# A transformer stack on one Trainium2 core: the first attention group's maximum products start two pairs later, and the second group's stack is loaded between stores

## The chip, the cores and the metric

One Trainium2 chip, one core. The metric is the device time of one execution in microseconds (us), taken as the median of several runs. The kernel before the change has a median of 1548.95 us over three runs (1544.71 to 1552.33).

## What is computed

Four attention blocks follow each other on x of shape (2, 1024, 256), with a context of 77 tokens a batch. The change touches the first block alone, and of it the projections and the first two groups of heads:

```python
b, t, d = x.shape                                     # 2, 1024, 256; 16 heads of width 16
qkv = (_ln(x, g1, be1) @ w_qkv + b_qkv).reshape(b, t, 3, h, dh)
ckv = (context @ w_ckv + b_ckv).reshape(b, s, 2, h, dh)
k = jnp.concatenate([k_self, k_ctx], axis=1)
v = jnp.concatenate([v_self, v_ctx], axis=1)
scores = jnp.einsum('bthd,bshd->bhts', q, k) * scale
scores = jnp.where((j >= t) | (j <= i), scores, -jnp.inf)   # causal on own keys, the context is always seen
attn = jax.nn.softmax(scores, axis=-1)
attn_out = jnp.einsum('bhts,bshd->bthd', attn, v).reshape(b, t, d)
x = x + attn_out
```

What follows (a feed-forward block, three attention layers over the context and themselves, a windowed attention and a last encoder layer) is left as it is.

## The kernel before, in words

The program is written engine by engine, with semaphores between the engines, and in stages: at the end of a stage every engine drains and waits for the others (`next_stage`). The stage of this change is the first, called the front here, and the beginning of the second, the attention of the first block (`at0`).

**The front** makes 18 *features* (q and k of the 2048 tokens and the keys of the context, each 128 features wide and up to 512 tokens long) and 18 *values* (v of 128 tokens each). They alternate: feature i and value i are pair i, and the items are numbered 0 to 35, feature i being number 2i. The table of TensorE's order is `front_tensor`, that of the others `front_scalar`, `front_vector`, `front_gpsimd` and `front_sync`.

- A feature is four matmul passes of 512 columns on TensorE (L570). ScalarE rounds it to bf16 (L607), VectorE takes the remainder (L642), ScalarE rounds that (L588), GpSimd takes what is still left (L681). The three bf16 parts lie in a ring of 6 buffers, and SyncE stores them to DRAM (L696). ScalarE waits for the buffer's earlier store.
- A value is four passes of 256 columns (L576), one addition on VectorE (L637) into a ring of 5 buffers, and a store (L699). VectorE waits for the buffer's earlier store.
- Into this are woven the transposes of the normalised x (L557, `TURNS_AT`, the last two at numbers 22 and 24).

**The maximum products.** The softmax of this kernel subtracts row maxima that are found beforehand. For each group of 4 heads there are 43 products of q and k (7 over the context, L1199, and 36 over the own keys, L1210) in banks 6 and 7 in turn: product n may start when VectorE has reduced product n-2 (`chunk_free`; L1427, L1438, L1442). A last transpose on TensorE (L1215) and four small VectorE instructions turn the maxima into three bf16 rows (`neg_max_parts`). SyncE sends these rows into the q stack of the group by DMA (L1066, `send_maximum_rows`), and the scores of the group (L1243) wait for them. For group 0 all 43 products lie in the front: from pair `MAXIMA_FROM // 2` on, `MAXIMA_EACH` of them a pair. `front_maxima(A, pair, place)` names the one of a place: place 0 stands before the feature product, place 1 behind it, place 2 behind the value product. Whatever is left comes after pair 17. VectorE follows the same table.

**The loads.** A group's stack (q, k and context keys, three parts each; pieces 0 to 2 of `load_group`, L1001 to L1004, nine DMAs) and its values (piece 3, L1007 and L1008) are read back from DRAM. Group 0's stack is asked for after number 9. Its values, all of group 1 and then the rows of group 0 are asked for at the end of the front, behind the last store. All of it goes through SyncE's one queue, in this order. Groups 2 and on, and the weights of the next blocks, follow in the next stage (`attention_sync`).

Of the kernel before, what the change touches and what calls it, by code (L numbers as in the profile page):

```python
# [182 lines left out]
def build(nc, a, out):  # L183
    with ExitStack() as ctx:
        program(nc, ctx, a, out)


def program(nc, ctx, a, out):
# [97 lines left out]
    def need(e, sem, value):  # L286

        if not (isinstance(value, int) and value <= 0):
            e.wait_ge(sem, value)
# [202 lines left out]
    def turn_ctx_tensor(e, s, src, ready=None, value=1):  # L492
        if ready is not None:
            e.wait_ge(ready, value)
        for b in range(B):
            for k in range(KT):
                e.transpose(PS[:, 6, (k * B + b) * P:(k * B + b) * P + SC], src[0:SC, b, k * P:(k + 1) * P],
                            ID[0:SC, 0:SC]).then_inc(s.turned, 1)
# [15 lines left out]
    RING, V_RING = len(P3), len(VT)  # L514

    def part(it, i, k):

        return P3[i % RING][:, 2 - k if it.reverse else k, 0:it.n]
# [2 lines left out]
    FRONT_SCR = [WA[:, 2560 + CH * i:2560 + CH * (i + 1)] for i in range(2)]  # L521
    TURNS_AT = {0: [(0, 0), (0, 1)], 2: [(1, 0)], 4: [(1, 1)], 14: [(2, 0)], 16: [(2, 1)], 22: [(3, 0)], 24: [(3, 1)]}
    STATISTICS_AT, NORMALISE_AT = {6: 2, 14: 3}, {8: 2, 16: 3}
    MAXIMA_FROM, MAXIMA_EACH = 20, 3

    def in_order(items):

        for i, (it, v) in enumerate(zip(*items)):
            yield True, it, i
            yield False, v, i  # L530

    def front_maxima(A, pair, place):

        items = numbered(A, 0, -1)[0]
        n = max(pair - MAXIMA_FROM // 2, 0) * MAXIMA_EACH
        if pair == len(items0[0]):
            return items[n:]
        return items[n + place:n + place + 1] if pair >= MAXIMA_FROM // 2 else []

    def turn_bank(n):  # L540

        return PS[:, (3, 7)[n % 2] if n < 4 else 3, :]

    def turn_needs(n):

        return n - 1 if n < 4 else 3 if n == 4 else n

    def front_tensor(e, s, tn, tnc, nm, items, A):

        turn_ctx_tensor(e, tnc, CTXN)  # L550
        for number, (is_feature, it, i) in enumerate(in_order(items)):
            for c, k in TURNS_AT.get(number, []):
                n = KT * c + k
                e.wait_ge(nm.normed, c + 1)
                need(e, tn.taken, turn_needs(n))
                for j in range(4):
                    m = e.transpose(turn_bank(n)[:, j * P:(j + 1) * P], FRONT_ROWS[:, 4 * c + j, k * P:(k + 1) * P], ID[:, :])  # L557
                m.then_inc(tn.turned, 1)
            if it.chunk is None:
                e.wait_ge(tnc.taken, 1)  # L560
                e.wait_ge(ld.w_ctx, 16)
            else:
                e.wait_ge(tn.taken, KT * (it.chunk + 1))
                e.wait_ge(ld.w0, 16)
            if is_feature:
                for x in front_maxima(A, i, 0):
                    attention_chunk(e, A, *x, 0, -1)
                need(e, s.left, i - 2)
                for j, (l, r) in enumerate(it.mms):
                    m = e.matmul(PS[0:P, i % 3, 0:it.n], l, r, start=(j == 0), stop=(j == len(it.mms) - 1))  # L570
                m.then_inc(s.product, 1)
            else:
                need(e, stored0.v_taken, i - 1)
                for sl, mms in it.mms:
                    for j, (l, r) in enumerate(mms):
                        m = e.matmul(PS[0:it.p, 4 + i % 2, sl], l, r, start=(j == 0), stop=(j == len(mms) - 1))  # L576
                m.then_inc(s.v_product, 1)
            for place in ((1,), (2,))[not is_feature]:
                for x in front_maxima(A, i, place):
                    attention_chunk(e, A, *x, 0, -1)  # L580
        for x in front_maxima(A, len(items[0]), 0):
            attention_chunk(e, A, *x, 0, -1)
# [36 lines left out]
    def front_vector(e, s, nm, items, A):  # L619

        statistics, scales, _ = ln_steps(e, nm, X, "layer", 1e-5, arrived=ld.x_chunks)

        def normalise_here(c):
            scales(c)
            e.drain()
            for t in range(4 * c, 4 * c + 4):
                z = e.tensor_scalar(FRONT_ROWS[:, t, :], X[:, t, :], RS[:, t:t + 1], NB[:, t:t + 1], ALU.mult, ALU.add)
            z.then_inc(nm.normed, 1)

        def value(v, i):  # L630
            e.wait_ge(s.v_product, i + 1)
            if i >= V_RING:
                e.wait_ge(value_stored[i % V_RING], 16 * (i // V_RING))
            dst = VT[i % V_RING][0:v.p, 0:512].rearrange("p (h w) -> p h w", w=32)[:, :, 0:16]
            src = PS[0:v.p, 4 + i % 2, 0:D].rearrange("p (h w) -> p h w", h=16)
            r = v.row[0:v.p, :].rearrange("p (h w) -> p h w", h=16)
            e.tensor_tensor(dst, src, r, ALU.add).then_inc(stored0.v_taken, 1)  # L637

        def remainder(it, i):
            e.wait_ge(s.first_part, i + 1)  # L640
            need(e, stored0.split, i - 1)
            e.scalar_tensor_tensor(RBUF[:, i % 2, 0:it.n], PS[:, i % 3, 0:it.n], it.bias, part(it, i, 0),  # L642
                                   ALU.add, ALU.subtract).then_inc(s.left, 1)

        def maxima(pair, place):
            for w, dg, k, n, bank in front_maxima(A, pair, place):
                e.wait_ge(A.s.chunk_ready, n + 1)
                if w in "AL":
                    maximum_part(e, A, k, n, bank, 0, FRONT_SCR, w == "L")
                else:  # L650
                    maximum_split(e, A, 0, bank)
        for c in range(2):
            statistics(c)
            normalise_here(c)
        e.wait_ge(ld.rows0, 16)
        late = []
        for number, (is_feature, it, i) in enumerate(in_order(items)):
            if number in STATISTICS_AT:
                statistics(STATISTICS_AT[number])
            if number in NORMALISE_AT:  # L660
                normalise_here(NORMALISE_AT[number])
            if number < MAXIMA_FROM:
                (remainder if is_feature else value)(it, i)
                continue
            if is_feature:
                maxima(i, 0)
            for make, *of in late:
                if make is (remainder if is_feature else value):
                    make(*of)
            late = [x for x in late if x[0] is not (remainder if is_feature else value)]  # L670
            late.append((remainder if is_feature else value, it, i))
            maxima(i, 2 - is_feature)
        for make, *of in late:
            make(*of)
        maxima(len(items[0]), 0)
# [7 lines left out]
    def stored_after(e, feat, val):  # L683

        for u in range(RING):
            need(e, part_stored[u], 16 * ((feat + RING - 1 - u) // RING))
        for u in range(V_RING):
            need(e, value_stored[u], 16 * ((val + V_RING - 1 - u) // V_RING))
# [13 lines left out]
    def ones_sync(e, A):  # L702

        e.dma_start(ONES_ROWS, ONEB[0:M_ROWS * A.nh * TB, :]).then_inc(A.s.ones, 16)
        e.wait_ge(A.s.ones, 16)
        for u in range(A.slots):
            e.dma_start(slot16(A, u)[1][K16:K16 + M_ROWS, :, P:P + T], ONES_ROWS.rearrange("(r h t) n -> r h (t n)", r=M_ROWS, h=A.nh))\
                .then_inc(A.s.ones, 16)

    def front_sync(e, items, A):  # L710

        ones_sync(e, A)
        for number, (is_feature, it, i) in enumerate(in_order(items)):
            store_item(e, is_feature, it, i)
            if number == 2 * FIRST_FEATURES - 1:
                e.wait_ge(A.s.cleared, 1)
                for u in range(FIRST_FEATURES):
                    e.wait_ge(part_stored[u], 16)
                load_group(e, A, 0, 0, (0, 1, 2))
        stored_after(e, len(items[0]), len(items[1]))  # L720
        e.wait_ge(A.s.ones, 16 * (1 + A.slots))
        load_group(e, A, 0, 0, (3,))
        load_group(e, A, 1, 1)
        send_maximum_rows(e, A, 0)

    def project(stage):
# [2381 lines left out]
    part_stored, value_stored = stored0.parts, stored0.values  # L3108
# [45 lines left out]
    def _(e):  # L3154
        nxt = lambda: next_stage(e, "sync")
        load_sync(e)
        nxt()
        front_sync(e, items0, at0)
        nxt()
        attention_sync(e, at0)  # L3160
# [204 lines left out]
```

## Time and profile before

| what | value |
| --- | --- |
| median of three runs | 1548.95 us (1544.71 to 1552.33) |
| the profiled execution's own time | 1548.56 us |
| its span in the trace | 1546.8 us |
| granted TensorE clock over the span | 0.94 of full speed |
| TensorE busy | 1333.0 us (86%) |
| VectorE busy | 1069.4 us (69%) |
| ScalarE busy | 739.4 us (48%) |
| GpSimd busy | 538.2 us (35%) |
| front and first rows, until group 0's first scores start | 103.38 us |

The busy shares are averages over stages with different limits. The part of interest is the first 110 us. The timeline of an engine gives for each row the start, the time and the instruction, and in brackets the idle time before it with what ended it. Adjacent rows overlap where instructions are pipelined: the distance between starts is what an instruction costs, the time in its row also holds its latency. A view by windows gives for each stretch the busy time of every engine, the granted clock as a share of full speed, the share of time that the 16 DMA engines were busy (it may pass 1.00 a little), and GB/s.

### The profile page before, as it was taken

Reading aid. Unit: us, or ns where it says so; the run is one execution under the profiler, and the core shown is the slowest. Engines: PE = TensorE matmul, PEld = TensorE weight load, DVE = VectorE, ACT = ScalarE, POOL = GpSimd, SP = SyncE. Lnnn points to the kernel's source line nnn. Section 1 sums busy time; section 2 is a strip of 40 time slices with the busy share of each in tenths; the row PEclk is TensorE's granted clock in tenths of the full one; section 3 lists DMA queues with packets and bytes.
Section 4 is the critical chain, followed back from the end, with each engine's and each line's share of the span. In section 5 each row is a group of like instructions: output and inputs, shape, how many; then the busy total and the mean of one; then the engine's idle time right before and its main releaser. Section 6 shows DMA issues by size and latency. Waiting matters only on the chain.

```text
span 1546.8 us, 21751 instructions
## 1 busy us (share of the span) xinstructions
PE 1333.0 (86%) x7242; PEld 768.5 (50%) x7242; DVE 1069.4 (69%) x2667; ACT 739.4 (48%) x1030; POOL 538.2 (35%) x462
## 2 busy tenths in 40 slices
PE   7859999998699879879999979799998789788897
PEld 4413333332388756644444356344433577445796
DVE  6558888886654377667577767675777888676654
ACT  4325565567776345523334445233443634245664
POOL 3211111112410042207876621267864257001212
PEclk9869999999899998979999999799999889799999
DMA  6794333300000001553430317704400020630001
GB/s 201 198 201 122 63 66 65 64 8 2 28 1 1 1 1 67 159 170 69 96 87 22 104 49 213 186 16 96 96 28 12 17 35 32 155 65 3 1 1 55
DMA packets 80022, 110.39 MB, mean 71 GB/s; under 512 B 16713, under 2 KB 55811, under 8 KB 78119
## 3 DMA queue, kind: packets, MB, share of 16 engines
q1 hardware_dynamic: 79910, 109.00, 28.6%
q8 instruction: 58, 0.95, 0.3%
q14 instruction: 54, 0.43, 0.1%
HBM read 70.62 MB, written 37.83 MB: 70 GB/s over the span
## 4 chain that ended last, share of the span: by engine, by line
PE 41%; POOLq 19%; DVE 16%; issue 12%; ACT 6%; DVEq 3%; DMA 2%; SPq 1%; POOL 1%; ACTq 0%
POOLq L1157 18%; PE banks L1268 6%; PE banks L1610 5%; PE banks L1625 5%; PE banks L1210 4%; PE banks L1243 3%; PE banks L2196 3%; PE banks L2226 2%; DVE mask_rows L1438 1%; PE banks L570 1%; PE banks L1221 1%; DVE max_parts L1442 1%; PE banks L2744 1%; DVE max_parts L1427 1%; ACT x_feat L1403 1%
## 5 line engine op out<-in xcount | busy, mean ns | idle before, releaser
L1403 ACT ACTIVATE x_feat<-banks,key_bias 128x1024 f32<-128x1024 f32 x160 | 176.6, 1114 | 266.9 <-PE banks L1250 210.8
L1156 POOL TENSOR_TENSOR x_feat<-x_feat 128x1024 f32<-128x1024 f32 (+1 forms) x112 | 243.1, 2170 | 98.3 <-ACT x_feat L1403 90.1
L1210 PE MATMUL banks<-stacks 128*128 128x512 f32 (+4 forms) x640 | 225.1, 400 | 35.7 <-DVE max_parts L1431 12.2
L1268 PE MATMUL banks<-x_feat,v_group 128*32 128x512 f32 (+4 forms) x1312 | 232.6, 571 | 8.3 <-ACT x_feat L1403 4.7
L1403 ACT ACTIVATE x_feat<-banks 128x1024 f32<-128x1024 f32 (+2 forms) x224 | 178.8, 841 | 112.2 <-PE banks L1243 111.1
L1210 PEld LDWEIGHTS banks<-stacks 96*128 96x128 bf16 (+1 forms) x640 | 79.1, 139 | 219.0 <-DVE max_parts L1431 90.8
L1243 PE MATMUL banks<-stacks 99*128 99x512 bf16 (+3 forms) x512 | 131.2, 347 | 23.1 <-ACT x_feat L1403 12.3
L1180 POOL TENSOR_SCALAR_AFFINE_SELECT x_feat<-x_feat 128x256 f32<-128x256 f32 x128 | 53.4, 420 | 249.2 <-ACT x_feat L1403 247.5
L1431 DVE CUSTOM_DVE_ANT_0 scratch<-banks,mask_rows 128x512 f32<-128x512 f32 x128 | 88.1, 689 | 51.4 <-PE banks L1210 51.2
L1249 PE MATMUL banks<-stacks 128*128 128x512 f32 x256 | 111.5, 436 | 9.5 <-DMA stacks<-neg_max_parts_r 9.5
L1610 PE MATMUL banks<-stacks 128*128 128x512 f32 x384 | 102.7, 407 | 9.8 <-DVE stacks L1592 8.9
L1250 PE MATMUL banks<-stacks 96*128 96x512 f32 x256 | 103.8, 405 | 0.0
L1625 PE MATMUL banks<-stacks 128*128 128x256 f32 x768 | 102.1, 284 | 0.0
L1625 PEld LDWEIGHTS banks<-stacks 128*128 128x128 f32 x768 | 99.1, 191 | 3.9
L1442 DVE TENSOR_REDUCE max_parts<-banks 128x1 f32<-128x512 f32 x128 | 84.4, 687 | 12.7 <-PE banks L1210 11.8
L1427 DVE TENSOR_REDUCE max_parts<-banks 128x5 f32<-128x385 f32 (+2 forms) x104 | 54.0, 547 | 45.0 <-PE banks L1199 30.0
L1431 DVE CUSTOM_DVE_ANT_0 w_even<-banks,mask_rows 128x512 f32<-128x512 f32 x112 | 77.0, 688 | 11.6 <-PE banks L1210 11.3
L1610 PEld LDWEIGHTS banks<-stacks 128*128 128x128 f32 x384 | 71.1, 197 | 23.3 <-issue 9.6
L2196 PE MATMUL banks<-x_feat,w_odd 128*128 128x512 f32 x160 | 80.6, 632 | 0.8 <-ACT x_feat L2315 0.8
L1268 PEld LDWEIGHTS banks<-x_feat,v_group 128*32 128x32 f32 (+1 forms) x1312 | 41.5, 119 | 78.3 <-issue 53.1
L1249 PEld LDWEIGHTS banks<-stacks 128*128 128x128 f32 x256 | 50.0, 195 | 60.3 <-issue 42.6
L1243 PEld LDWEIGHTS banks<-stacks 99*128 99x128 bf16 x512 | 44.9, 99 | 61.4 <-ACT x_feat L1403 29.5
(308 smaller groups left out, 2461.8 us busy)
## 6 DMA issues: line engine op xcount, KB each, us to landing
stacks<-q_parts_r SPq DMA_DIRECT2D x18, 512.0 KB, 7.1
stacks<-k_parts_r SPq DMA_DIRECT2D x18, 512.0 KB, 10.7
q_parts_r<-stacks SPq DMA_DIRECT2D x16, 512.0 KB, 3.1
k_parts_r<-stacks SPq DMA_DIRECT2D x16, 512.0 KB, 3.4
v_group<-v SPq DMA_DIRECT2D x14, 512.0 KB, 15.1
stacks<-q_parts SPq DMA_DIRECT2D x16, 384.0 KB, 5.1
stacks<-q_parts SPq DMA_DIRECT2D x16, 256.0 KB, 7.4
w_even<-in_w SPq DMA_DIRECT2D x4, 1024.0 KB, 16.0
```

The costliest lines, as they stand in the source:

```text
L1156: e.tensor_tensor(total, total, p, ALU.add)
L1157: e.drain().then_inc(s.tile_summed, 1)
L1210: m = e.matmul(PS[:, bank, at:at + wide], q[0:rows, h, qt * P:(qt + 1) * P], keys[0:rows, h, k0:k0 + wide], start=True, stop=True, skip_gr ...
L1243: m = e.matmul(o, k[0:rows, head_of_k(A, r, h), k0:k0 + P], q[0:rows, h, qs], start=True, stop=True, skip_group_check=True)
L1249: e.matmul(o, ka[:, hk, ks], qa[:, h, qs], start=True, stop=False)
L1250: m = e.matmul(o, kb[0:96, hk, ks], qb[0:96, h, qs], start=False, stop=True)
L1268: m = e.matmul(PS[w * h:w * (h + 1), bank, t.q0:CH], V[:, h, :], PB[:, t.index % 2, h // 2, h % 2, 0:CH - t.q0], start=t.first, stop=t.las ...
L1403: e.activation(dst, PS[:, 2 * (st % 2):2 * (st % 2) + 2, 0:CH - t.q0], ACT.Exp, scale=A.scale, bias=bias).then_inc(s.p_ready, 1)
L1431: e.tensor_tensor_reduce(scratch, PS[:, bank, :], MB[:, k0:k0 + CH], 1.0, LOWEST, ALU.add, ALU.max, maxp[:, h, qt, half:half + 1]).then_in ...
L1610: mm = e.matmul(PS[:, i % 3, :], w[:, k, ms], x[:, c % 2, k, :], start=k == 0 and w is w1h and x is XH, stop=k == KT - 1 and w is w1l)
L1625: mm = e.matmul(o, h[:, i % 4, ts], w[:, m, :], start=m == 0 and t % 2 == 0 and h is HID_H and w is w2h, stop=m == MT_F - 1 and h is HID_L ...
L2196: m = e.matmul(PS[:, n % 2, :], left, right, start=k == 0, stop=k == KT - 1)
```

## The change

Two tables of numbers change: the maximum products start at pair 12, four a pair (places 2 and 3 both stand behind the value product), where they started at pair 10, three a pair. 24 of the 43 lie in the pairs before and after. And SyncE asks for the three pieces of group 1's stack after the stores of numbers 24, 27 and 30, for group 0's values after number 32; at the end only group 1's values stand between the last store and the rows of group 0.

```diff
-    MAXIMA_FROM, MAXIMA_EACH = 20, 3
+    MAXIMA_FROM, MAXIMA_EACH = 24, 4
...
-            for place in ((1,), (2,))[not is_feature]:
+            for place in ((1,), (2, 3))[not is_feature]:
                 for x in front_maxima(A, i, place):
                     attention_chunk(e, A, *x, 0, -1)
...
-            maxima(i, 2 - is_feature)
+            for place in ((1,), (2, 3))[not is_feature]:
+                maxima(i, place)
...
+    NEXT_STACK_AT, FIRST_VALUES_AT = (24, 27, 30), 32
...
+            if number in NEXT_STACK_AT:
+                load_group(e, A, 1, 1, (NEXT_STACK_AT.index(number),))
+            if number == FIRST_VALUES_AT:
+                for u in range(V_RING):
+                    e.wait_ge(value_stored[u], 32)
+                load_group(e, A, 0, 0, (3,))
         stored_after(e, len(items[0]), len(items[1]))
         e.wait_ge(A.s.ones, 16 * (1 + A.slots))
-        load_group(e, A, 0, 0, (3,))
-        load_group(e, A, 1, 1)
+        load_group(e, A, 1, 1, (3,))
         send_maximum_rows(e, A, 0)
```

TensorE's order from pair 10 on, before. L570 is a feature product, L576 a value product, L557 a transpose of x, L1199 a maximum product over the context (up to five small matmuls):

```order
26 L576 MATMUL banks<-w_even,x_feat 128x256 x2
27 L1199 MATMUL banks<-stacks 128x77 x5
28 L570 MATMUL banks<-x_feat,w_even 128x512 x2
29 L1199 MATMUL banks<-stacks 128x77 x5
30 L576 MATMUL banks<-w_even,x_feat 128x256 x2
31 L1199 MATMUL banks<-stacks 128x77 x5
```

and in the changed kernel, where L1199 has become L1207:

```order
26 L576 MATMUL banks<-w_even,x_feat 128x256 x2
27 L570 MATMUL banks<-x_feat,w_even 128x512 x2
28 L576 MATMUL banks<-w_even,x_feat 128x256 x2
29 L557 MATMUL banks<-ident,w_even 128x128 x4
30 L570 MATMUL banks<-x_feat,w_even 128x512 x2
31 L576 MATMUL banks<-w_even,x_feat 128x256 x2
32 L557 MATMUL banks<-ident,w_even 128x128 x4
33 L1207 MATMUL banks<-stacks 128x77 x5
```

The first product that reads group 0's stack stood ahead of pair 10 and now stands ahead of pair 12: two features, two values and both last transposes have moved in front of it.

TensorE's order around pair 14, before (L1210 is a maximum product over own keys):

```order
44 L570 MATMUL banks<-x_feat,w_even 128x512 x2
45 L1210 MATMUL banks<-stacks 128x512
46 L576 MATMUL banks<-w_even,x_feat 128x256 x2
47 L1210 MATMUL banks<-stacks 128x512 x2
48 L570 MATMUL banks<-x_feat,w_even 128x512 x2
```

and in the changed kernel (L1218 is what L1210 was):

```order
43 L570 MATMUL banks<-x_feat,w_even 128x512 x2
44 L1218 MATMUL banks<-stacks 128x512
45 L576 MATMUL banks<-w_even,x_feat 128x256 x2
46 L1218 MATMUL banks<-stacks 128x512 x3
47 L570 MATMUL banks<-x_feat,w_even 128x512 x2
```

Between a value product and the next feature product stood two maximum products, and now stand three, in two banks.

SyncE's order at the end of the front, before:

```order
56 L699 DMA v<-v_group 128x4x128 [waits set2_40]
57 L1007 DMA v_group<-v 128x1024 [waits set2_34,set2_35,set2_33,set2_36,set2_32,set2_37,set2_31,set2_38,set2_30,set2_27,set2_29,set2_28]
58 L1008 DMA v_group<-v 77x128
59 L1001 DMA stacks<-q_parts 48x4096
...
67 L1004 DMA stacks<-kctx_parts 16x4x77
68 L1007 DMA v_group<-v 128x1024
69 L1008 DMA v_group<-v 77x128
70 L1066 DMA stacks<-neg_max_parts 1x32x128 [waits set2_8,set2_18,set2_15]
```

and in the changed kernel:

```order
67 L700 DMA v<-v_group 128x4x128 [waits set2_40]
68 L1015 DMA v_group<-v 128x1024 [waits set2_34,set2_35,set2_33,set2_36,set2_32,set2_37,set2_31,set2_38,set2_30,set2_27,set2_29,set2_28]
69 L1016 DMA v_group<-v 77x128
70 L1074 DMA stacks<-neg_max_parts 1x32x128 [waits set2_8,set2_18,set2_15]
```

Eleven DMAs that stood between the last store and group 0's rows have moved up among the stores; two are left there.

## Rows read from the trace of the kernel before

**Rows 1.** Chain of waits in order of time: start us, us, what

```profile
40.00 7.89 DMA stacks<-kctx_parts
...
94.86 0.29 DVE neg_max_parts L1466
...
96.55 6.69 DMA stacks<-neg_max_parts
103.38 1.03 PE banks L1243 x2
```

**Rows 2.** Timeline of TensorE, around pairs 8 to 10, 12 to 14 and 17

```profile
34.99 0.60 PE L557 MATMUL banks<-ident,w_even 128*128 128x128 f32 x4
35.43 1.88 PE L570 MATMUL banks<-x_feat,w_even 128*128 128x512 f32 x4
...
38.01 1.88 PE L570 MATMUL banks<-x_feat,w_even 128*128 128x512 f32 x4
39.73 1.03 PE L576 MATMUL banks<-w_even,x_feat 128*128 128x256 f32 x4
48.02 0.48 PE L1199 MATMUL banks<-stacks 96*128 96x77 bf16 x5 [7.27 <-DMA stacks<-kctx_parts]
...
58.05 1.96 PE L570 MATMUL banks<-x_feat,w_even 128*128 128x512 f32 x4
...
61.36 1.88 PE L570 MATMUL banks<-x_feat,w_even 128*128 128x512 f32 x4
63.08 0.38 PE L1210 MATMUL banks<-stacks 96*128 96x512 bf16 x1
63.30 1.03 PE L576 MATMUL banks<-w_even,x_feat 128*128 128x256 f32 x4
64.16 0.60 PE L1210 MATMUL banks<-stacks 96*128 96x512 bf16 x2
...
74.35 1.88 PE L570 MATMUL banks<-x_feat,w_even 128*128 128x512 f32 x4
```

**Rows 3.** Timeline of VectorE: one pair's share, and four products of the tail

```profile
63.50 0.69 DVE L1442 TENSOR_REDUCE max_parts<-banks 128x1 f32<-128x512 f32 x1 [0.21 <-PE banks L1210]
64.11 0.41 DVE L637 TENSOR_TENSOR v_group<-banks,rows_even 128x256 f32<-128x256 f32 x1
...
69.21 0.74 DVE L642 SCALAR_TENSOR_TENSOR y_tok<-banks,cols,y_tok 128x512 f32<-128x512 f32 x1
...
80.56 2.87 DVE L1442 TENSOR_REDUCE max_parts<-banks 128x1 f32<-128x512 f32 x4
```

**Rows 4.** Windows: PE, PEld, DVE, ACT, POOL busy, PEclk, DMA share, GB/s

```profile
40.00:84.00 44.00, 34.22 (x140) 18.21 (x138) 28.85 (x73) 12.96 (x21) 11.54 (x10) 0.84 0.75 207
85.00:105.00 20.00, 8.03 (x24) 2.02 (x25) 9.10 (x35) 0.52 (x1) 2.05 (x4) 0.50 1.04 181
```

**Rows 5.** The instructions of L1066, the rows' DMAs, over the whole program

```profile
DMA to landing us min/median/max: 1.7/1.8/6.7
```

**Rows 6.** Timeline of SyncE's queue: start and time of an issue

```profile
81.34 0.53 SPq L699 DMA_DIRECT2D v<-v_group  x1
89.95 0.42 SPq L1007 DMA_DIRECT2D v_group<-v  x1
...
95.24 1.91 SPq L1066 DMA_DIRECT2D stacks<-neg_max_parts  x3
```

**Rows 7.** DMA issues at 41.7 to 42.2 us: KB each, us to landing

```profile
v<-v_group SPq DMA_DIRECT2D x1, 256.0 KB, 7.9
```

**Rows 8.** Windows as in rows 4: where the granted clock falls or stays

```profile
55.00:75.00 20.00, 20.00 (x84) 11.53 (x83) 17.10 (x43) 8.23 (x14) 6.46 (x6) 1.00 0.62 193
78.00:80.00 2.00, 0.39 (x1) 0.10 (x1) 2.00 (x9) 0.63 (x1) 0.95 (x2) 1.00 0.67 200
80.00:82.00 2.00, 1.60 (x3) 0.30 (x3) 1.90 (x7) 0.00 (x0) 0.91 (x1) 0.62 0.93 288
1368.00:1412.00 44.00, 36.28 (x392) 18.43 (x392) 29.23 (x74) 21.29 (x20) 0.00 (x0) 1.00 0.20 40
```

## The prediction

> **What bounds the kernel now.** The page gives TensorE 86% of the span and VectorE 69%, but the change touches only the first 104 us, so the chain of waits of that stretch comes first [rows 1]. The reader is to see two DMAs in it: TensorE stands until 48.02 for the last piece of group 0's stack, and again until 103.38 for the three bf16 rows of the maxima, whose last DMA needs 6.69 us. Next comes TensorE's timeline [rows 2], for the first wait (7.27 us) and for what a pair costs, then VectorE's [rows 3] for its share. SyncE's queue and the landing times [rows 5 to 7] show what stands in front of the rows. The windows [rows 4, 8] show how full the DMA engines are, and when the granted clock falls.
>
> The front is one chain: TensorE and VectorE share its end, the attention starts only when it is over, and a group's start depends on the one before. Nothing later waits for a fixed time. I therefore take whatever moves the first scores (103.38) as moving the end of the kernel by the same amount.
>
> **Part 1, the start of the products.** From row to row a feature costs TensorE 1.72 us (38.01 to 39.73), a maximum product over own keys 0.22 (63.08 to 63.30), a value 0.86 (63.30 to 64.16), a group of four transposes 0.44 (34.99 to 35.43) [rows 2]. Value 9 ends at 39.73 + 0.86 = 40.6. Instead of standing until 48.02, TensorE now does pairs 10 and 11 and both last transposes: 2 x 2.58 + 2 x 0.44 = 6.0 us, to 46.6. Then it meets the same wait, now 1.4 us, since the loads of group 0 are issued where they were. The first product starts at 48.0 again and feature 12 at 48.2, where it started at 58.05: **9.85 us earlier**. In this are the 7.27 us of wait and the slow start after it, when TensorE's granted clock was at the half level, 1.2 GHz.
>
> Some of it is paid back at once. VectorE does value 10 before its first maximum, and value 10 and 11 wait for the stores of values 5 and 6, which are issued right behind the loads. That of value 6 goes out at 41.7 to 42.2 and lands 7.9 us after its issue [rows 7], at about 50, and that of value 5 some 1 us before it. I charge pairs 12 and 13 (seven of their eight products are the short ones over the context) with 3.9 and 3.7 us, where pair 12 took 3.31 (58.05 to 61.36) and pair 13 some 3.25: **+1.0 us**.
>
> **Part 2, four products a pair.** The number inside the pairs stays 24, the tail after pair 17 stays 20. In the four pairs 14 to 17 TensorE's own work grows to 1.72 + 0.86 + 4 x 0.22 = 3.46 us, from the 3.25 that a pair took ((74.35 - 61.36) / 4). But the order counts more. Three products now stand in a row between the value and the next feature, in two banks. The third may start when VectorE has reduced the first of them: that reduction starts 0.42 us behind its product (63.08 to 63.50), takes 0.69, and some 0.05 passes until TensorE goes on [rows 2, 3]. So from the first of the three to the end of the wait are 1.16 us, where there were 0.44, and a pair is 1.72 + 0.22 + 0.86 + 0.22 + 0.22 + 0.72 of waiting and first slot: 2.80 + 1.16 = 3.96. VectorE has 0.66 for the remainder (69.21's row, without its latency), 0.33 to 0.41 for the value and four times some 0.65: 3.6 to 3.7 at best. It arrives a little late at the first of the three, because the value's addition stands in front. I take 4.2. The bounds are 3.6 (VectorE never idle) and 4.5 (both engines' waits added). Over four pairs that is 4 x (4.2 - 3.25) = **+3.8 us**, between +1.4 and +5.0.
>
> The tail is 20 products paced by VectorE at about 0.7 each (2.87 for four, [rows 3]) before and after: no change. So the maxima of group 0 are ready 9.85 - 1.0 - 3.8 = **5.0 us earlier**, between 3.8 and 7.4, at about 90.1 instead of 95.1 (94.86 + 0.29, [rows 1]).
>
> **Part 3, the loads.** Before, eleven DMAs with 0.5 MB of group 0's values and 1.6 MB of group 1's stack, then 0.5 MB of group 1's values, were in the queue when the rows were issued at 95.24 [rows 6], and the DMA engines were busy throughout at 181 GB/s [rows 4]: 2.7 MB take about 15 us, from 84.66 to 99.6 at best. The rows, 8 KB each, landed after 6.69 us, while the median of all rows' DMAs is 1.8 [rows 5]. With only group 1's values in front, issued right behind the last stores, I take 1.8 for the last of them: **4.9 us earlier**, between 0 and 4.9.
>
> What the nine plus two moved DMAs cost where they now stand: SyncE spends about 0.45 us on each issue, some 5 us in all over 25 us, which delays a store by 1.4 us at most at a time. Features 12 to 17 wait for no store from there on, since their buffers' next turn would be feature 18. Values 15 to 17 wait for those of values 10 to 12, ten microseconds older. The DMA engines are the tight place: 44 us at a share of 0.75 are 33 us of work before [rows 4], and 2.1 MB at 181 GB/s add 12, so 45 us of work stand in the 39 us that the front now has until its last store. The last stores then land some 5 us late, at about 85, and group 1's values at about 88, still ahead of the rows at 90. I charge nothing, but the cover is only 2 us.
>
> **Sum**, against the profiled execution's own 1548.56 us: -5.0 - 4.9 = -9.9, which gives 1538.66, said as **1538.7 us**. The median of the runs, 1548.95, is 0.4 higher, so it serves as well.
>
> **The rivals.**
>
> *The rows stay late.* The oversubscribed DMA engines have not finished when the rows are issued, or group 2's load, issued right behind the rows as before, slows them. For it: the 45 us against 39, and the minimum cover of 2 us. Against it: the other groups' rows also have the next load right behind them and need 1.8 us. The time: only part 1 and 2 count, 1548.56 - 5.0 = 1543.6.
>
> *The clock falls in the pairs: slower than before.* The change takes TensorE from wholly busy (20.00 of 20 us, clock 1.00) to some 83% busy with a wait in each pair. Between 78 and 80 it was busy for 0.39 of 2 us, and from 80 on the clock came down to the half level, 1.2 GHz [rows 8]. At that level the work of a pair doubles to 6.9 us and, with the longer latencies, to about 7.6. From pair 12 on that would be 4 x 3.4 + 2 x 2 = 17.6 us more than in part 2, and 1548.56 - 9.9 + 17.6 = 1556.3. It decides from about the third slow pair on. Against it: from 1368 to 1412 TensorE was busy 36.28 of 44 us, 82%, with waits of the same kind on VectorE, and the clock stayed at 1.00 [rows 8]. The Trainium skill has a rule that speaks for this rival: its page TensorE: Matmul & The Clock Gate, section A second HAM failure mode: psum-queue depth-cycling, describes a kernel that cycled through banks, idled briefly between groups of matmuls and had its clock swing between the two levels. By that rule the time would be the rival's; the row at 82% disagrees, and I follow the row.
>
> *The gain is taken back behind the front.* The next stage, or a later one, ends on something that did not move, and the total stays at 1547 to 1549. For it speaks nothing that I see in the chain; against it, every later wait is on work of this same program.
>
> **How the numbers follow.** Both gains in full or nearly so (1536 to 1541.5): 0.60. Rows late: 0.20, 1543.6. Gain taken back or both terms small: 0.12, 1546 to 1549. Clock falls: 0.08, 1556.3. The forecast's own bounds are 1548.56 - 7.4 - 4.9 = 1536.3 and, with late rows, 1548.56 - 3.8 = 1544.8. The runs of before lie up to 4 us from their median, so the range is 1535 to 1546. About 0.5%, 7.7 us, is what a measurement can tell from no change here; the line is at 1541.2. Faster by more than that: most of the first case (1538.7 and below counts wholly, some of its upper part does not) and a quarter of the second, 0.60. Within 0.5%: 0.33. Slower: the last case, 0.07.
>
> **What the changed profile would show.** Right: the wait for group 0's stack is 1 to 2 us and stands ahead of feature 12 at 48; pairs 14 to 17 are 4.1 to 4.3 us apart, with a wait of some 0.7 us for a maximum ahead of each feature, at clock 1.00; the last of the four small instructions behind the maxima ends at 90; the rows land 1.8 us after their last issue and the first scores start at 93 to 94; the end of the kernel has moved by the same. Wrong: a landing of 4 us or more (rows late), a granted clock of 0.5 between 50 and 70 (clock), a wait of VectorE or ScalarE on a store behind pair 13, or a first score at 93 with an end above 1545.

## The result, and the profile after

The changed kernel's median is 1533.01 us over 5 runs (1530.10 to 1539.63), beside 1546.70 us of the kernel before (5 runs, 1543.30 to 1552.33): ratio 0.9918, 95% interval 0.9896 to 0.9940. It is faster, as forecast, but by more than forecast, and the time lies below the range of 1535 to 1546. The profiled execution's own time is 1534.61 us, its span 1532.9, against 1548.56 and 1546.8 before. Two more sets of runs of the same kernel gave the ratios 0.9924 (0.9902 to 0.9946) and 0.9944 (0.9926 to 0.9962).

The chain of waits of the changed kernel, start us, us, what. Line numbers have moved by up to 8:

```profile
38.84 9.53 DMA stacks<-kctx_parts
48.51 0.34 PE banks L1207 x5
...
92.29 1.84 DMA stacks<-neg_max_parts
94.27 1.02 PE banks L1251 x2
```

Against [rows 1] the load of group 0's stack is still in the chain, now with the transposes and four items done beside it. The last of the rows' DMAs takes 1.84 us, where it took 6.69. The first scores start at 94.27 instead of 103.38: 9.1 us.

TensorE's timeline, from pair 9 to pair 14:

```profile
39.70 1.03 PE L576 MATMUL banks<-w_even,x_feat 128*128 128x256 f32 x4
40.56 1.88 PE L570 MATMUL banks<-x_feat,w_even 128*128 128x512 f32 x4
...
46.16 0.60 PE L557 MATMUL banks<-ident,w_even 128*128 128x128 f32 x4
48.51 0.34 PE L1207 MATMUL banks<-stacks 96*128 96x77 bf16 x5 [1.75 <-DMA stacks<-kctx_parts]
48.68 1.96 PE L570 MATMUL banks<-x_feat,w_even 128*128 128x512 f32 x4
...
52.85 1.96 PE L570 MATMUL banks<-x_feat,w_even 128*128 128x512 f32 x4
...
56.71 1.88 PE L570 MATMUL banks<-x_feat,w_even 128*128 128x512 f32 x4
58.43 0.38 PE L1218 MATMUL banks<-stacks 96*128 96x512 bf16 x1
58.65 1.03 PE L576 MATMUL banks<-w_even,x_feat 128*128 128x256 f32 x4
59.51 0.60 PE L1218 MATMUL banks<-stacks 96*128 96x512 bf16 x2
60.77 0.38 PE L1218 MATMUL banks<-stacks 96*128 96x512 bf16 x1 [0.66 <-DVE max_parts L1450]
60.98 1.88 PE L570 MATMUL banks<-x_feat,w_even 128*128 128x512 f32 x4
...
69.62 1.88 PE L570 MATMUL banks<-x_feat,w_even 128*128 128x512 f32 x4
```

The wait for the stack has shrunk from 7.27 us [rows 2] to 1.75. Feature 12 starts at 48.68 (58.05 before), feature 17 at 69.62 (74.35 before). The third product in a row waits 0.66 us for VectorE ahead of the next feature: there are four such waits, of 0.66, 0.74, 0.66 and 0.66 us, ahead of features 15, 16 and 17 and at the beginning of the tail, and pairs 14 to 16 take (69.62 - 56.71) / 3 = 4.30 us each.

SyncE's queue at the end of the front:

```profile
77.30 0.63 SPq L700 DMA_DIRECT2D v<-v_group  x1
82.68 0.34 SPq L1015 DMA_DIRECT2D v_group<-v  x1
83.08 0.37 SPq L1016 DMA_DIRECT2D v_group<-v  x1
90.99 1.88 SPq L1074 DMA_DIRECT2D stacks<-neg_max_parts  x3
```

and the windows, columns as in [rows 4]:

```profile
57.00:74.00 17.00, 14.28 (x54) 7.42 (x52) 14.54 (x41) 4.82 (x8) 4.89 (x5) 1.00 1.05 260
80.00:90.00 10.00, 6.91 (x17) 1.25 (x15) 8.97 (x36) 0.00 (x0) 0.00 (x0) 0.50 0.29 91
```

The stores and loads fill the DMA engines from 57 to 74 (share 1.05; it was 0.62 from 55 to 75, [rows 8]). The last stores land 5.4 us after their issue at 77.3: the next issue, which waits for them, starts at 82.68. Before it was 3.3 us (81.34 in [rows 6] to an issue at 84.66). Group 1's values are asked for 7.9 us ahead of the rows. From 80 to 90 the DMA engines have a share of 0.29, and from 86 on, when those values have landed, they stand idle. TensorE is 84% busy from 57 to 74 and its granted clock stays at 1.00.

So all of the forecast is in the picture, and 9.1 us of the 13.9 between the two spans. The other 4.8 lie behind the first scores: from there to the end it was 1443.4 us before and 1438.6 now, in code that the change does not touch. That was the first question for the runs.

### The profile page after: what moved, and what is told of

Same layout as the page of the kernel before. It is cut to its first block, busy times and chain, and to the rows that moved or that the text cites. A ratio compares the mean times of both kernels' runs of the same rounds, so it can differ in the third digit from the quotient of the medians.

```text
span 1532.9 us, 21753 instructions
## 1 busy us (share of the span) xinstructions
PE 1328.7 (87%) x7242; PEld 766.8 (50%) x7242; DVE 1068.3 (70%) x2667; ACT 739.0 (48%) x1030; POOL 538.3 (35%) x462
## 4 chain that ended last, share of the span: by engine, by line
PE 40%; POOLq 19%; DVE 16%; issue 11%; ACT 6%; DVEq 3%; DMA 2%; SPq 1%; POOL 1%; ACTq 0%
POOLq L1165 19%; PE banks L1276 6%; PE banks L1618 5%; PE banks L1633 5%; PE banks L1218 4%; PE banks L2204 3%; PE banks L1251 3%; PE banks L2234 2%; DVE max_parts L1450 1%; DVE mask_rows L1446 1%; PE banks L1229 1%; ACT x_feat L1411 1%; DVE max_parts L1435 1%; PE banks L2222 1%; DVE scratch L1446 1%
## 5 line engine op out<-in xcount | busy, mean ns | idle before, releaser
L1218 PE MATMUL banks<-stacks 128*128 128x512 f32 (+4 forms) x640 | 224.2, 399 | 37.1 <-DVE max_parts L1439 12.4
L1218 PEld LDWEIGHTS banks<-stacks 96*128 96x128 bf16 (+1 forms) x640 | 78.8, 138 | 219.5 <-DVE max_parts L1439 91.8
L1439 DVE CUSTOM_DVE_ANT_0 w_even<-banks,mask_rows 128x512 f32<-128x512 f32 x112 | 77.0, 688 | 10.8 <-PE banks L1218 10.7
```

What stands on the lines that cost most here:

```text
L1218: m = e.matmul(PS[:, bank, at:at + wide], q[0:rows, h, qt * P:(qt + 1) * P], keys[0:rows, h, k0:k0 + wide], start=True, stop=True, skip_gr ...
L1439: e.tensor_tensor_reduce(scratch, PS[:, bank, :], MB[:, k0:k0 + CH], 1.0, LOWEST, ALU.add, ALU.max, maxp[:, h, qt, half:half + 1]).then_in ...
```

## The experiments

### The same two kernels again: does the part behind the front belong to the change?

No edit. The kernel before, with 12 runs of its own:

> The kernel before, unchanged, profiled and timed once more. Two theories on the 13.9 us between the two spans (1546.8 and 1532.9), of which the first scores of group 0 account for 9.1 (103.38 and 94.27). Theory A, chance episodes: the other 4.8 us are stretches at the half clock behind 1050 us (near 1060, 1124 and 1340) that differ from execution to execution. Then this profile has its first scores at 103.4 within 0.3, but the distance from the first scores to the end differs from the 1443.4 us of before by more than 1 us, the stretches of low clock behind 1050 us are not the same ones, and the runs' times follow their mean granted clock (a higher clock, a shorter time). Theory B, the change's own later gain: the distance from first scores to end is a property of the kernel, 1443.4 within 0.5 us again, with the same stretches of low clock. Ratio to before 1.000 within 0.002 by both.

Median 1546.42 us, ratio 0.9995 (0.9976 to 1.0015). The span of its profile was 1540.7 us, 6.1 less than the first profile of the same program. Yet its first scores came later:

```profile
106.61 1.01 PE L1243 MATMUL banks<-stacks 99*128 99x512 bf16 x2 [12.00 <-DMA stacks<-neg_max_parts]
```

The distance from the first scores to the end was therefore 1434.1 us, against 1443.4. One kernel draws numbers 9.3 us apart here, twice the 4.8 in question. The windows, columns as in [rows 4], show what differs. Here is a stretch of the first attention at the same distance behind the first scores, in the first profile:

```profile
383.38:398.38 15.00, 11.05 (x62) 2.72 (x54) 7.92 (x20) 14.42 (x23) 1.62 (x4) 0.89 0.00 0
```

and in this one:

```profile
386.61:401.61 15.00, 10.30 (x63) 2.28 (x62) 8.21 (x24) 14.96 (x23) 1.63 (x4) 1.00 0.00 0
```

The granted clock (0.89 against 1.00 of full speed) was at its half level for some 3 us in one execution and not in the other. The time at the half level behind the first scores, added up over windows of 5 us as twice (1 - clock) times 5 (the last window is not a full one), was 154.7 us in the first profile and 134.5 in the second. Over the 12 runs the time follows the mean clock: 1540.54 to 1544.74 us at 0.942 to 0.945, 1548.10 to 1552.02 us at 0.935 to 0.940. Theory A holds and theory B falls. Two parts of its text failed. The episodes do not lie only behind 1050 us: some 15 of the 20 us of half clock that the two profiles differ by lie ahead of it, like the stretch shown. And the first scores were not at 103.4 within 0.3, but 3.2 us later. The load of group 0 had landed 0.8 us later and the rows took 12.0 us instead of 9.8.

The changed kernel, with 6 runs:

> The changed kernel, unchanged, profiled and timed once more. Theory A (chance episodes): first scores at 94.3 within 0.3; distance from there to the end is another one than 1438.6 us, and over all runs the ratio to before comes near 1 - 9.1/1547 = 0.994. Theory B (a later gain that belongs to the change): the distance is again 1438.6 within 0.5, and the ratio again near 1 - 13.9/1547 = 0.991.

Median 1536.92 us, ratio 0.9924. First scores at 94.43, distance to the end 1442.4 us where the first profile had 1438.6: again theory A. The ratio lies between the two forecasts and tells nothing alone.

A third profile of each:

> The kernel before once more, one look. The wait for the rows was 9.8 us in its first profile and 12.0 us in its second. If it is a fixed 9.8 with one outlier, this one shows 9.8 within 0.3; if it varies with how the queue drains, anything from 9.5 to 12.5. Distance from first scores to the end: 1434 to 1444 us, and it follows the time at the half clock behind the first scores (154.7 us gave 1443.4, 134.5 us gave 1434.1: 0.46 us for each).

Time 1548.95 us, span 1547.2; the wait for the rows:

```profile
105.07 0.59 PE L1243 MATMUL banks<-stacks 99*128 99x512 bf16 x1 [10.70 <-DMA stacks<-neg_max_parts]
```

So this wait varies, 9.8, 12.0 and 10.7 us. Distance to the end 1442.1 us at 161.7 us of half clock; my factor of 0.46 us for each would have given 1446.6. Over all ten profiles at hand by then the distance rises by about 0.30 us for each microsecond at half clock, with a correlation of 0.91: it follows, not one for one.

> The changed kernel again, for more runs. If the gain is what the first scores show (105.0 us as a mean of three profiles of before: 103.38, 106.61, 105.07; 94.35 of two of the changed kernel), the ratio to before is near 1 - 10.7/1547 = 0.993, and first scores are at 94.3 again. If another part of the kernel gains as well, the ratio stays at 0.991 or below.

Median 1537.33 us (6 runs), ratio 0.9944. First scores:

```profile
93.50 1.01 PE L1251 MATMUL banks<-stacks 99*128 99x512 bf16 x2 [4.92 <-DMA stacks<-neg_max_parts]
```

The wait for the rows is 4.90, 4.93 and 4.92 us in the three profiles of the changed kernel: it no longer varies. The first scores are at 105.0 us (mean of three) before and at 94.1 now, 10.9 apart, and the distance from them to the end has the same mean in both, 1439.9 us before and 1439.7 now. All runs of the sets together have a mean of 1546.3 us before (67 runs, standard deviation 3.1) and of 1535.7 us now (17 runs, 3.3): 10.6 apart. The first scores' shift explains the whole change within the scatter.

### The two halves apart

Products as changed, loads as before (the edit against the kernel before, in part):

```diff
-    MAXIMA_FROM, MAXIMA_EACH = 20, 3
+    MAXIMA_FROM, MAXIMA_EACH = 24, 4
...
         load_group(e, A, 0, 0, (3,))
         load_group(e, A, 1, 1)
         send_maximum_rows(e, A, 0)
```

> Maximum products as in the changed kernel (from pair 12, four a pair), loads of group 0's values and of group 1 at the end as before. Theory of the two terms: pairs 14 to 17 are 4.3 us apart, the maxima are ready at 90.9, 4.2 us earlier than before (95.1), and the rows still land 6 to 7 us after the last issue, since the last store is some 4 us earlier as well and the queue ahead of them is the same: first scores at 99.2, gain 4.2 us, ratio 0.997. Rival (queue is not it): with these products the rows land in 1.8 us, first scores at 94.3. Rival that the half clock between 75 and 100 us carries part of the gain: first scores at 97 or less with rows still 6 us late.

Median 1540.67 us (8 runs), ratio 0.9957 (0.9937 to 0.9976). The end of the maxima and the first scores:

```profile
89.16 0.37 PE L1218 MATMUL banks<-ident,max_rows 128*32 128x128 f32 x1 [1.30 <-DVE max_rows L1450]
100.66 1.01 PE L1246 MATMUL banks<-stacks 99*128 99x512 bf16 x2 [11.13 <-DMA stacks<-neg_max_parts]
```

The last transpose behind the maxima starts at 89.16 as in the changed kernel (89.00); it was at 93.23, 94.24 and 94.00 in the three profiles of before, 93.8 in the mean. TensorE waits 11.1 us for the rows, the queue being what it was. Pairs 14 to 16 are 4.3 us apart. The first scores are 1.5 us later than forecast, because the last of the rows' DMAs took 8.08 us and not 6 to 7. Both rivals fall: the order of the products does nothing for the rows, and the half clock of the tail hides no gain.

Loads as changed, products as before (again against the kernel before, in part):

```diff
+            if number in NEXT_STACK_AT:
+                load_group(e, A, 1, 1, (NEXT_STACK_AT.index(number),))
...
         load_group(e, A, 1, 1, (3,))
         send_maximum_rows(e, A, 0)
```

> Loads as in the changed kernel, maximum products as before (from pair 10, three a pair). Theory of the two terms: TensorE waits 7.3 us for group 0's stack, the maxima are ready at 95.1 within 0.5, and the rows land 1.8 us after their last issue instead of 6.7: first scores at 98.5, gain 4.9 us, ratio 0.997. Rival (DMA engines overfull): pairs 12 to 17 are longer than 3.25 us because stores land late, and the maxima are ready at 96.5 or later. If theories of both terms hold, the two gains add up to the 9.1 of the changed kernel.

Median 1537.02 us (6 runs), ratio 0.9938 (0.9918 to 0.9958).

```profile
92.94 0.37 PE L1223 MATMUL banks<-ident,max_rows 128*32 128x128 f32 x1 [1.31 <-DVE max_rows L1455]
98.23 1.01 PE L1251 MATMUL banks<-stacks 99*128 99x512 bf16 x2 [4.92 <-DMA stacks<-neg_max_parts]
```

First scores at 98.23, forecast 98.5. Features 13 to 17 start 3.25 us apart (61.06 to 74.05 us), as before, and VectorE, ScalarE and GpSimd wait for no DMA from 38 to 90 us: the added 2.1 MB of loads among the stores delay no engine. They do delay the stores. The last of them is issued at 81.91 and has landed at 89.24 (81.34 and 84.66 before), but no engine needs it earlier. The rival of overfull DMA engines falls. The ratio of 0.997 was forecast from the first profile's rows and lies outside the interval; the gain is larger, because the rows of before waited longer in the other profiles.

Against the mean of before the first scores are 4.4 us earlier for the products alone and 6.8 for the loads alone, 11.2 together, and 10.9 for both: by the first scores the two terms add up. The runs' means do not show it as well. They are 6.1, 8.5 and 10.6 us below that of before, with a standard error of about 1 us each, so the halves sum to 4 us more than the whole.

### What is in front of the rows?

Against the changed kernel:

```diff
-            if number in NEXT_STACK_AT:
-                load_group(e, A, 1, 1, (NEXT_STACK_AT.index(number),))
...
-        load_group(e, A, 1, 1, (3,))
+        load_group(e, A, 1, 1)
         send_maximum_rows(e, A, 0)
```

> The changed kernel with group 1's stack asked for at the end again, behind the last store and ahead of the rows; group 0's values stay moved up. Theory (the rows wait for the bytes in front of them in the queue): with 2.7 MB asked for from 84.66, 85.70 and 80.54 on, the rows landed at 103.2, 106.5 and 100.5, that is 18.5 to 20.8 us later; 2.15 MB in front of them take 15 to 16.5 us from 82.2 on, so first scores at 97 to 99. Rival one (it is group 0's values that held the rows): first scores at 94.3. Rival two (it is only the stack, however much else is there): first scores at 100.5.

Median 1540.86 us (12 runs), ratio 0.9965 (0.9949 to 0.9980).

```profile
98.25 1.01 PE L1249 MATMUL banks<-stacks 99*128 99x512 bf16 x2 [8.44 <-DMA stacks<-neg_max_parts]
```

First scores at 98.25, within 97 to 99. The wait is 8.4 us with 2.15 MB in front, 9.8 to 12.0 with 2.7, and 4.9 with 0.55 that have time to land. From the first of these issues to the landing of the rows it was 15.9 us with 2.15 MB and 18.6 to 20.8 with 2.7. The rows wait for the bytes ahead of them in SyncE's queue, and neither the stack nor the values alone hold them.

The bytes in front are not the whole of it. Here is the kernel before, first profile, from the first of the issues to the landing of the rows:

```profile
84.66:103.24 18.58, 6.49 (x16) 1.24 (x15) 9.30 (x36) 0.00 (x0) 2.05 (x4) 0.50 1.01 181
```

At 181 GB/s this is 3.4 MB, 0.7 more than stood in front, so part of group 2's load, issued behind the rows, was moved before they had landed. With an empty queue in front, the same load behind them does no harm (1.84 us in the changed kernel). How much it adds when the queue is full was not tried.

### Is the bank wait or VectorE the bound of a pair?

Three products a pair (the same change of places follows in VectorE's table):

```diff
-    MAXIMA_FROM, MAXIMA_EACH = 24, 4
+    MAXIMA_FROM, MAXIMA_EACH = 24, 3
...
-            for place in ((1,), (2, 3))[not is_feature]:
+            for place in ((1,), (2,))[not is_feature]:
...
```

> The changed kernel with three products a pair from pair 12 (18 in the pairs, 26 behind them with the transpose). Theory (bank wait, and VectorE's total work, set the end of the front): pairs are 3.25 us apart again, without a wait ahead of the feature, the tail has six more products of 0.7 us, and the maxima are ready at 90.0, 0.9 us earlier than with four a pair: first scores at 93.4. Rival (as many products as possible belong into the pairs): the maxima are ready at 92 or later.

Median 1537.17 us (8 runs), ratio 0.9947 (0.9927 to 0.9968).

```profile
87.13 0.37 PE L1223 MATMUL banks<-ident,max_rows 128*32 128x128 f32 x1 [1.31 <-DVE max_rows L1455]
92.43 1.01 PE L1251 MATMUL banks<-stacks 99*128 99x512 bf16 x2 [4.93 <-DMA stacks<-neg_max_parts]
```

First scores at 92.43: a microsecond earlier than I forecast for it, and 1.6 us earlier than the changed kernel's mean of 94.1. Some 0.4 us of the 1.6 are group 0's stack, which landed earlier in this profile: feature 12 starts at 47.99, against 48.38 in the changed kernel's mean. By the rest, 1.2 us, the fourth product a pair is a small loss: the 1.05 us that it adds to a pair is more than the 0.7 us of a product in the tail. The runs do not show so little (means of 1536.9 and 1535.7 us).

Four a pair, but spread out (the first and second piece of the edit are in TensorE's table, the last in VectorE's):

```diff
                 for j, (l, r) in enumerate(it.mms):
                     m = e.matmul(PS[0:P, i % 3, 0:it.n], l, r, start=(j == 0), stop=(j == len(it.mms) - 1))
+                    if j == 0:
+                        for x in front_maxima(A, i, 1):
+                            attention_chunk(e, A, *x, 0, -1)
...
-            for place in ((1,), (2, 3))[not is_feature]:
+            for place in ((2,), (3,))[not is_feature]:
...
-            for place in ((1,), (2, 3))[not is_feature]:
+            for place in ((1, 2), (3,))[not is_feature]:
```

> The changed kernel with the four products of a pair spread out: one ahead of the feature product, one between its two halves, one behind it, one behind the value product, so that no three stand in a row in two banks. Theory (the 4.3 us of a pair come from the bank wait ahead of each feature, 0.66 to 0.74 us, and not from VectorE being full): pairs 14 to 17 are 3.6 us apart, the maxima are ready at 88.1 or earlier (90.9 in the changed kernel), first scores at 91.5, so 2.8 us less than the changed kernel. Rival (VectorE is the bound of a pair at 4.3): pairs stay at 4.2 or more, first scores at 94.

Median 1532.74 us (6 runs), ratio 0.9919 (0.9897 to 0.9942). TensorE's timeline over a pair:

```profile
63.17 1.02 PE L570 MATMUL banks<-x_feat,w_even 128*128 128x512 f32 x2
64.03 0.38 PE L1221 MATMUL banks<-stacks 96*128 96x512 bf16 x1
64.25 1.02 PE L570 MATMUL banks<-x_feat,w_even 128*128 128x512 f32 x2
65.11 0.38 PE L1221 MATMUL banks<-stacks 96*128 96x512 bf16 x1
65.33 1.03 PE L579 MATMUL banks<-w_even,x_feat 128*128 128x256 f32 x4
66.19 0.63 PE L1221 MATMUL banks<-stacks 96*128 96x512 bf16 x2
66.66 1.02 PE L570 MATMUL banks<-x_feat,w_even 128*128 128x512 f32 x2
```

and its windows:

```profile
57.00:70.00 13.00, 12.99 (x52) 7.12 (x51) 13.00 (x38) 4.82 (x8) 3.68 (x4) 1.00 1.05 246
```

The pairs take 3.54 us (features 14 to 17 start from 56.03 to 66.66), without a wait worth a bracket, and now both engines are wholly busy: 12.99 and 13.00 of 13 us. First scores at 91.07, forecast 91.5. In the changed kernel the wait for the bank was the bound of the pair, not VectorE; at 3.54 us there is no idle time left on either engine.

> The spread order again, on the same chip as the changed kernel. First scores at 91.1, as in its first profile, 3.3 us ahead of the changed kernel. If all of that reaches the end, the median is 3 us below that of the changed kernel, within the 2 us or so that such medians scatter, and the ratio to before is near 1 - 14/1547 = 0.991. If the front's gain is taken back by what follows, the two medians are the same.

Median 1531.30 us (6 runs), ratio 0.9917 (0.9895 to 0.9940), first scores at 91.33. Beside it on the same chip the changed kernel had 1537.33 and 0.9944: the medians are 6.0 us apart where 3 were forecast, and the intervals of the two ratios overlap. Over both sets the spread order's mean is 1532.9 us (12 runs), 2.8 below the 1535.7 of the changed kernel, and its first scores are 2.9 us ahead. By the first scores it is ahead of the changed kernel and of the one with three products a pair; by the runs alone the 2.8 us have a standard error of about 1.2.

## Why the prediction was right or wrong

**The shift of the first scores is the shift of the end: right, in the mean.** 10.9 us there, 10.6 in the means of the runs. Two single profiles of one kernel break it by up to 9 us, and the prediction used one as if it were the kernel.

**Part 1, feature 12 9.85 us earlier: nearly right.** 9.4 us between the two first profiles (58.05 to 48.68), because the stack landed 0.5 us later in the second. Pairs 12 and 13 took 4.17 and 3.86 us, forecast 3.9 and 3.7. As forecast, VectorE did stand for the store of value 5, until 48.79 us:

```profile
48.79 0.42 DVE L637 TENSOR_TENSOR o_feat<-banks,rows_even 128x256 f32<-128x256 f32 x1 [4.84 <-DMA v<-o_feat]
```

**Part 2, a pair of 4.2 us: right in mechanism, the number in part by luck.** It measured 4.30, with the wait ahead of the feature that the sum named. But the sum of 3.96 leaves out the third product's own 0.22 us behind its wait. With it the sum is 4.18, and VectorE's lateness, for which 4.2 was taken, is only the 0.10 us by which the first of the three to the end of the wait took 1.26 (59.51 to 60.77) and not 1.16. The maxima were 5.0 us earlier by the mean of three profiles each (last transpose 93.8 and 88.8), which is the forecast; between the two first profiles, for which it was made, it was 4.2. That the means agree is luck too: feature 12 came 10.3 us earlier there and not 9.85, and what was paid back behind it was 5.2 us and not 4.8.

**Part 3, the rows 4.9 us earlier: right in mechanism, too small in size.** This is the term that was mis-sized. The wait after the maxima was 9.8 us in the one profile that I had, and 12.0 and 10.7 in the next two, 10.8 in the mean. After the change it is 4.9 every time. The term is 5.9 us, not 4.9. The prediction gave it the bounds 0 and 4.9, as if the profiled landing of 6.69 us were the worst that the queue ahead of it could do. Behind 2.7 MB the last of the rows' DMAs took 6.69, 8.94, 7.63 and 8.08 us in four profiles: it has no fixed landing time there, and the bound should have been open above.

**The cover of 2 us: right to be there, larger than said.** The last stores landed at 82.7, not 85, and group 1's values had landed by 86, not 88, 5 us ahead of the rows' issue at 90.99.

**The step that put the time outside the range** is, besides that term, the sentence that the median of 1548.95, three runs, "serves as well". The forecast of 1538.66 was 5.7 us above the measured 1533.01, and this splits in three. The kernel before has a mean of 1546.3 us over 67 runs, with single runs from 1539.8 to 1552.3, and my base of 1548.56 was 2.3 us above it. The gain was 10.6 us and not 9.9: another 0.7, and the rows' term, too small by 1.0, is the one in the sum that accounts for it. The changed kernel's five runs, with a median of 1533.0, lay 2.7 us below its mean of 1535.7: that part is chance. Against the mean of all its runs the changed kernel would have been inside the range. The range's lower end took the best case of the sum and left 1.3 us for the runs, where the executions of one kernel differ by 12.

**The rivals.** Rows late: no, 1.84 us. Clock falls in the pairs: no; from 57 to 74 us TensorE was 84% busy with a wait of 0.7 us in each pair, and the granted clock was 1.00. The rule of the Trainium skill that was cited for this rival (TensorE: Matmul & The Clock Gate, A second HAM failure mode: psum-queue depth-cycling) does not show here. Gain taken back behind the front: no; the distance to the end is 1439.9 us before and 1439.7 now, in the means of three.

What stays open is why an episode of half clock comes in one execution and not in the next of the same program; the profiles show that it does, and not what decides it. It was also not tried whether the 4.9 us left between the maxima and the first scores can be shortened, of which 1.3 us pass from the first to the third of the issues in series and 1.8 from there to the landing of the last.

## What to carry to other kernels

Look at what is queued in front of a small, late transfer that everything waits for: with megabytes ahead of it that could have gone earlier, it lands only when they are through, and how late that is varies from execution to execution (9.8 to 12.0 us here, 4.9 without them). When work is woven into a chain of products through two banks, space it so that the bank is free when its turn comes: the same four products cost 4.3 us a pair in a row of three and 3.5 spread out. And before forecasting a difference of a per cent, ask how far single executions of the kernel lie apart, and centre the forecast on many of them rather than on the profiled one.

## What the runs showed of the hardware that was not expected

The distance from the first scores to the end, some 7,000 matmuls in the same order, took between 1433.7 and 1443.4 us in twelve profiles, and between 134 and 162 us of it lay at the half clock in the ten where I added it up. The wait for three transfers of 8 KB behind 2.7 MB took 9.8, 11.1, 10.7 and 12.0 us in four profiles, and 4.89 to 4.93 in all with a short queue. SyncE's own issue of a store took 4.71 us at 41.58 in the changed kernel (3.07 us before), where most take 0.4 to 0.5. It stands behind the nine DMAs of group 0's stack, 1.6 MB, and that issue took 3.1 to 4.7 us in all twelve profiles. The issue of L328, behind group 2's load and two of 1 MB each, took 6.8 to 10.9. So an issue behind much queued work can hold up SyncE itself; what sets the time of such an issue is not shown.
